# VectorE normalises the rows two batches ahead at a turn's end, and two copies become maxima of a tensor with itself

## What is computed

```
xn = _layernorm(x, axis=-1)
x = x + _L0_attn_ref(xn, ...) + _L0_ffn_ref(xn, ...)
```

```
Qp = relu(Q / |Q| @ projection) + YAT_EPS
Kp = relu(K / |K| @ projection) + YAT_EPS
KV = einsum('bhsf,bhsd->bhfd', Kp, V)
QKV = einsum('bhsf,bhfd->bhsd', Qp, KV)
out = (QKV / max(Qp . K_sum, 1e-6)) @ Wo + bo
```

## Time and profile before

| | |
|---|---|
| median of three runs | 1308.59 us |
| the profiled execution | 1309.03 us |
| its span, first to last instruction | 1307.4 us |
| TensorE busy | 1172.8 us, 90% of the span |
| VectorE busy | 888.1 us, 68% |
| ScalarE busy | 621.7 us, 48% |
| GpSimd busy | 715.3 us, 55% |
| mean granted TensorE clock | 0.946 |

### The profile page before, as it was taken

One profiled execution on the slowest core, in us unless ns is written; L12 is line 12 of the kernel. 1 busy time (PEld: TensorE's weight loads), 2 busy tenths in 40 slices (PEclk: granted clock), 3 DMA queues, 4 the chain that ended last, 5 costly groups with the idle time before them and its releaser, 6 DMA issues.

```text
span 1307.4 us, 38053 instructions
## 1 busy us (share of the span) xinstructions
PE 1172.8 (90%) x14176; PEld 942.0 (72%) x14176; DVE 888.1 (68%) x1986; ACT 621.7 (48%) x1101; POOL 715.3 (55%) x702
## 2 busy tenths in 40 slices
PE   4888888888888888489999999999999999999996
PEld 2555555555565656268888888888888888888885
DVE  7888888888878885847666666665555555555542
ACT  3676767676857676333334444432233333322221
POOL 3323556655655557755555655555555555555451
PEclk9979798989888989589999999999999999999998
DMA  3422222222222121047776677655455555555440
GB/s 100 107 34 82 35 83 35 77 40 83 35 67 34 35 35 34 2 133 156 171 144 150 148 154 148 137 109 103 95 102 101 98 101 106 104 101 102 72 74 7
DMA packets 222412, 115.50 MB, mean 88 GB/s; under 512 B 156609, under 2 KB 215874, under 8 KB 222242
## 3 DMA queue, kind: packets, MB, share of 16 engines
q1 hardware_dynamic: 189410, 77.77, 25.1%
q0 software_dynamic: 32288, 34.78, 16.2%
q10 hardware_dynamic: 544, 0.52, 0.1%
HBM read 61.56 MB, written 52.35 MB: 87 GB/s over the span
## 4 chain that ended last, share of the span: by engine, by line
PE 55%; POOL 1%; issue 1%; DMA 1%; DVE 0%; POOLq 0%; ACT 0%
PE bank L1006 28%; PE bank L1023 27%; POOL slot_table L1131 1%; DMA xg<-xn_split,mt 0%; DMA out_dram<-area,mt 0%; DMA mt<-slot_table 0%; POOL out_dram L1230 0%; POOL xg L1223 0%; POOLq L1211 0%; DVE area L1624 0%; DVE area L1627 0%; PE bank L990 0%; ACT area L679 0%; POOLq L1207 0%; POOLq L1213 0%
## 5 line engine op out<-in xcount | busy, mean ns | idle before, releaser
L1006 PE MATMUL bank<-area 128*128 128x256 f16 (+1 forms) x3408 | 375.7, 268 | 2.9 <-issue 1.6
L1023 PE MATMUL bank<-area 128*128 x3240 | 365.3, 273 | 0.0
L1006 PEld LDWEIGHTS bank<-area 128*128 x3408 | 323.8, 98 | 45.3 <-issue 5.3
L1023 PEld LDWEIGHTS bank<-area 128*128 128x128 f16 x3240 | 316.4, 98 | 37.7 <-issue 0.2
L1230 POOL DMA_INDIRECT out_dram<-area,mt x135 | 219.0, 1622 | 183.3 <-ACT area L679 153.5
L1644 DVE TENSOR_SCALAR area<-area 128x512 f16<-128x512 f32 (+1 forms) x284 | 126.8, 447 | 278.8 <-ACT area L669 275.2
L669 ACT ACTIVATE area<-bank 128x512 f32<-128x512 f32 (+1 forms) x284 | 163.6, 576 | 183.7 <-PE bank L1006 181.5
L1646 DVE SCALAR_TENSOR_TENSOR area<-area 128x512 f16<-128x512 f32 (+1 forms) x284 | 189.8, 668 | 9.8
L679 ACT ACTIVATE area<-bank,mt 128x256 f32<-128x256 f32 x135 | 57.1, 471 | 288.8 <-PE bank L1023 288.8
L1131 POOL DMA_INDIRECT slot_table<-area x128 | 136.3, 1065 | 99.1 <-PE bank L869 39.5
L1223 POOL DMA_INDIRECT xg<-xn_split,mt x135 | 136.8, 1013 | 42.7 <-issue 40.5
(11 more groups left out here) (203 smaller groups left out, 1411.5 us busy)
## 6 DMA issues: line engine op xcount, KB each, us to landing
turned_rows<-xg SPq DMA_DIRECT2D x252, 64.0 KB
w_hl<-turned_rows SPq DMA_DIRECT2D x63, 256.0 KB, 3.1
area<-in_x_dram SPq DMA_DIRECT2D x16, 512.0 KB, 4.7
xn_split<-area SPq DMA_DIRECT2D x128, 64.0 KB, 2.2
w_raw<-in_w_dram SPq DMA_DIRECT2D x64, 128.0 KB
out_dram<-area SPq DMA_DIRECT2D x30, 256.0 KB, 3.7
area<-in_w_dram SPq DMA_DIRECT2D x14, 512.0 KB, 5.0
xg<-xn_split,mt POOLq DMA_INDIRECT x135, 3.4
```

The costliest lines, as they stand in the source:

```text
L1006: mm = nc.tensor.matmul(big[j][:, i2 * n:(i2 + 1) * n], we[:, bass.ds(e * EXPERT + (k * 2048 + wl * 1024 + c * P), P)], moe_xT[t % XT][:, ...
L1023: mm = nc.tensor.matmul(yb[:, a * D:(a + 1) * D], hT[u % 2][:, c, hl, a * P:(a + 1) * P], we[:, bass.ds(e * EXPERT + off, D)], start=(c == ...
```

## The change

Three edits. `normalise_rows(b+1)` at the start of a body turn stays only in turn 0. At the end of body turns 0 to 5 `normalise_rows(b+2)` now stands between `out_drain(b, 1)` and `v_over_norm(b+1, 1)`. The copy in `v_over_norm` and the cast in `kv_build` are written as the maximum of the tensor with itself, a TENSOR_TENSOR with two inputs in SBUF.

```
@@ v_over_norm
             ch.link(v.reciprocal(rn, norm[:, half, :, 2:4, :]))
-            ch.step(v.tensor_copy(dst[:, :, :, HD:HD + 1], rnf))
+            ch.step(v.tensor_tensor(dst[:, :, :, HD:HD + 1], rnf, rnf, ALU.max))
@@ kv_build
-            v.tensor_copy(kv_hl[:, 0], kvf).then_inc(kvf_ready, 1)
+            v.tensor_tensor(kv_hl[:, 0], kvf, kvf, ALU.max).then_inc(kvf_ready, 1)
@@ dve_turn
             choose(dve, b)
-            if body:
+            if first:
                 normalise_rows(dve, b + 1, 0)
                 normalise_rows(dve, b + 1, 1)
...
             out_drain(dve, phase, b, 1, first)
             if body:
+                if b + 2 < B:
+                    normalise_rows(dve, b + 2, 0)
+                    normalise_rows(dve, b + 2, 1)
                 v_over_norm(dve, b + 1, 1, chp)
```

## The result

The changed kernel takes 1314.87 us (median of 13 runs, 1309.31 to 1322.78), the kernel before 1307.87 us (median of 13, 1305.86 to 1311.08). The ratio is 1.0055, with an interval of 1.0042 to 1.0067: 7.2 us slower, give or take 1.7. I had forecast no measurable change.

What follows compares the result with a forecast made beforehand. First-stage waits: VectorE for GpSimd's refinement (21.4 us), TensorE for VectorE's KV-sum copy (9.2 us). Profiled 1309.03 minus 1.9 plus 1.1 gives 1308.2, median about 1307.8: no measurable change; 8-in-10 range 1303.8 to 1311.0.

Steps and rivals of the forecast that it cites:

- edit 2: Normalising at the end of turns 0 to 5: 2.67 us into 2.58 us idle, reciprocal at most 0.1 us later, cost 0.
- third rival: Normalising and GpSimd's refinement hold each other at the turn's end; reciprocal up to 2.2 us late, 1313 us; chance 0.07.
- the slack of 0.73: End of turn: values' multiplication ends at 121.58, waiting `kv_sum` of tile 4 starts 0.73 us later, so small delays cost nothing.
- Edit 1: Normalising out of the start of turns 1 to 6: each turn's A to E falls to about 18.82 us, 1.9 us gained.
- the sum of 1.9 us: Gain over turns 1 to 6 from removing normalising at their start, from each turn's difference to 18.82 us.
- A to E: Measure of a turn: from ScalarE's first query ReLU (A) to the start of `attend` of tile 4 (E), 18.62 to 19.90 us.
- where the gain stops: Turn's start: an earlier VectorE runs into GpSimd's `x_low` and is held at line 1439 until A + 5.48.
- edit 3: The two maxima: line 1439 held by `x_low`, 0.13 us more in six turns, 0.14 in two, 1.1 us lost.
- The first rival: The maxima get past GpSimd, so `kv_build` in turns 1 to 6 is not held: 1300 us; chance 0.09.
- the fourth rival: TensorE's wait for line 1507's copy just goes, saving 9.2 us: 1299 to 1300; shares the first rival's chance, 0.09.

Runs made afterwards that it cites:

- half_hole_again: Kernel before with four normalising instructions in the hole and four left at the turn's start, copies kept: 1309.75 us beside 1308.45, ratio 1.0006.
- move_third: Kernel before with only the normalising moved, both copies kept, on a chip of 1308.64: 1312.88 us, ratio 1.0021.
- fill_pointer: Kernel before plus eight extra two-scalar tensor_scalar in the hole of turns 0 to 5: 1314.25 us beside 1308.45, ratio 1.0048.
- fill_bnstats: Kernel before plus eight extra bn_stats in the hole of turns 0 to 5: 1309.29 us beside 1308.45, ratio 1.0005.
- the forms: Kernel before plus eight extra instructions in each turn's hole, another of six instruction forms per turn: 1352.08 us beside 1356.38, one run.
- maxima_only: Kernel before with only the two copies written as maxima, normalising not moved: 1354.83 us beside 1356.38, ratio 0.9994.
- the repeats on one chip: The change and the normalising move without maxima, rerun side by side against the kernel before at 1356.06 us: ratios 1.0030 and 1.0029.
- The first run of the move: Kernel before with only the normalising moved, both copies kept: 1352.49 us beside 1356.38, ratio 0.9965.

## Why the prediction was wrong, point by point

**The failed step is edit 2,** "I take 0", and what stands behind it, the third rival's "Against it": I had read from 404 ns for 256 elements and one SBUF tensor that the eight "stream one element per cycle" and "have no use for a second port", and so that GpSimd would not hold them. In the hole they took 6.51 us instead of 2.67, and so the conclusion is wrong. The reading under it isn't safe either: the same instruction takes 0.29 us with constants and 0.34 with one scalar, so the 404 ns can as well be two elements at a time and two scalars.

The rival itself was right in kind, and its price of 1313 near the 1314.87, but it got there by another way, the refinement's steps: it said that the reciprocal would be up to 2.2 us late, and it was 3.76. Of these, 1.44 came back, since line 1378 is no longer held (0.29 us in place of 1.73), which leaves 2.3 at the end of the values and, by the slack of 0.73 that I had named, 1.6 per turn. Line 838 shows 1.5 to 1.7 us in the rows above. Six times that is 9.4 us. The boundaries lost 6.1, of which the last, which the change doesn't touch, gained 2.1 with its higher clock; the six that it touches lost 8.1. They don't lose alike: the matmul starts 0.15 us behind the end of line 1379 in turns 1, 2, 3 and 6, but in turn 2 it has waited only 0.7 us, and in turns 4 and 5 TensorE waited for something else.

I had looked for the contention in the wrong neighbour too. I asked what the refinement's steps of 0.5 us would do; they stretch an instruction by 0.2 us at most. It is `v_total`, right behind them, with its 2.43 and 1.27 us, that costs the most. The hole ends where `v_total` starts. Of the first six, three take 0.62 us and two 0.45 or 0.46, and that is enough for the last two to fall into it. Four of them don't (half_hole_again).

The Trainium skill (SBUF — State Buffer, Who interferes with whom) says that a VectorE instruction with at most one SBUF input, outside the two-port modes, doesn't contend with GpSimd. Taken with the 404 ns, that was my conclusion. The 2.454 us of such an instruction beside line 1085 contradict the rule only if the instruction is outside those modes, and I had nothing but the 404 ns for that. The 341 ns with one scalar speak against it. If the normalising form is in a two-port mode, which the third rival named as the way in which it "would come true", rule and trace agree; the statistics, which ran free, fit the rule either way.

**Edit 1** gained less than it should, and the sum of 1.9 us was mis-sized. I expected A to E to shrink by 1.9 us less the maxima's 0.8 in these turns, so to 113.7. Without the maxima it is 113.91 (move_third) and 113.17 with half of the move, so 0.9 and 1.6 us gained; with the maxima 114.85. But fill_pointer, which keeps the normalising at the start, has 113.84 as well, though its copy of line 1507 comes 0.1 to 1.9 us behind A in every turn. The reason is the one that I had given for where the gain stops, taken further. Line 1439 ends at A + 5.64 in all six turns of fill_pointer and of move_third, held by `x_low`, and so it does in four of the six before. Only in turns 1 and 3 before does it end later, by 0.2 and 0.7 us. So a VectorE that comes earlier could gain 0.9 us, and not the 1.9 that I had from the differences between turns, and the 0.8 that edit 3 takes back leaves about nothing. The stretches scatter in single executions: by the same count fill_bnstats should have 114.2, and it has 115.90.

**Edit 3** came true where I had put it. Line 1439 as a maximum takes 2.10 us beside `x_low`, as in the first timeline (132.04 plus 2.10, so 134.14), and `x_low` ends at 131.72 plus 2.12, so 133.84:

```profile
131.72 2.12 POOL L1080 TENSOR_TENSOR area<-area 128x1024 f16<-128x1024 f32 x1 [9.05 <-ACT area L574]
```

It ends 0.30 us behind, where I had said 0.29. The first rival, that a maximum of equals gets past GpSimd, is out: this row, and the 6.56 us of eight such maxima in the forms. A to E with and without the maxima differ by 0.94 us (114.85 less 113.91, one execution each), for which I had 0.8.

**The wait of line 1507** went as predicted in turns 1 to 6, and the copy starts before A in all six (127.60 against 128.37 in turn 1). The 6.9 us that went with it (9.2 less the 2.3 of turn 0) did not come back, as said against the fourth rival. The clock is no part of the loss in the sum: 0.90 and 0.89.

**What stays open.** On the chips near 1308 the change costs 1.0055 (1.0042 to 1.0067) and the move alone 1.0021 (1.0007 to 1.0035). These intervals don't touch, so the maxima seem to add some 4 us to the move, of which I can show about 1; by the medians the change costs 7.0 us and the move 4.2, so 2.8 us. The two were not measured side by side there. Against more than 1 us stand fill_pointer, which loses 1.0048 without any maximum, maxima_only with 0.9994, and the repeats on one chip, in which the move and the change lose alike. The first run of the move, 0.9965, contradicts its two others, and I have no cause for it.

Nor was it settled what in the normalising form brings the hold. One reading is the two-port mode, as for the form with constants and the copies, which are held too; for it speaks that the form with one scalar is too fast for one element per cycle. The other is that the scalars read from SBUF bring it about. No run tells them apart, since none had the form with its scalars elsewhere. That the statistics ran free is no matter of their writing only 6 elements: line 1448, with one input in SBUF and one in PSUM, writes 512, and all its 120 instructions before took 0.67 to 0.69 us, those beside `x_low` too. Why three chips take 48 us longer for the same kernel wasn't tried.

## What to carry to other kernels

A hole in an engine's timeline is only as long as it is for the form of instruction that is put there: look up who runs on the sharing engine in the hole and right behind it, and what the form does beside that. Where it never ran beside it in the trace, its time is no proof that it won't be held: an instruction with scalars per partition can take as long as one that streams one element per cycle without being one. Put eight copies of it in the hole and look, before moving anything, and time it beside the same form with constants. Leave the end of a hole empty if a long GpSimd instruction starts there and somebody waits for what follows, or put the work behind the one that is waited for.

## What the runs showed of the hardware

- `tensor_scalar` in float32 over 256 elements with one or two scalars per partition read from SBUF was held by GpSimd's `tensor_tensor` on SBUF, to its end. With two scalars it took 2.454 us beside a 128x1024 one and 1.427 beside a 128x512 one, where alone it takes 0.404; with one scalar 2.446 and 1.422, where alone it takes 0.341.
- Each scalar per partition added some 0.06 us: 0.286 us with two constants, 0.341 with one scalar, 0.404 with two.
- `bn_stats` over one SBUF tensor of the same size (401 to 427 ns) was not held by the same instruction, and did not lengthen it (2.36 us).
- A maximum of a tensor with itself is held as one of two tensors: eight took 6.56 us. Copies and `tensor_scalar` with constants (eight in 1.70 us when free) were held for 2.45 us when they met line 1085 already running. Where the constants' form was already under way as line 1085 began, it wasn't held, and line 1085 took 2.73 us.
- GpSimd hardly paid for the held form with two scalars: line 1085 took 2.43 us in place of 2.37, and line 1087 took 1.27. Beside VectorE's lines 1379 and 1341, with two SBUF tensors each, line 1087 had taken 2.24 before.
